# Query projection of the quantised attention layer: whole numbers in one TensorE pass, scales applied afterwards

## The chip, the cores and the metric

The kernel runs on one core of a Trainium2 chip. The metric is the device time of one execution in microseconds (us). Three executions of the kernel before took 3217.35, 3220.0 and 3231.76 us, so the median is 3220.0 us.

## What is computed

The kernel computes a stack of four gated blocks on `x` (2 x 512 tokens, 512 features). Each block adds a cross attention over a context of 2 x 1024 tokens and then a feed-forward layer. The change concerns the third attention layer (L2). There the tokens and the query weights are rounded to 8-bit steps ahead of the product:

```python
def _qdq(x):
    s = jnp.maximum(jnp.max(jnp.abs(x), axis=-1, keepdims=True) / 127.0, 1e-08)
    return jnp.clip(jnp.round(x / s), -127.0, 127.0) * s
q = _qdq(x) @ _qdq(wq).T + bq
kv = cond @ wkv.T + bkv
attn = jax.nn.softmax(jnp.einsum('bnhd,bmhd->bhnm', q, k) * scale, axis=-1)
o = jnp.einsum('bhnm,bmhd->bnhd', attn, v).reshape(B, N, C)
out = _qdq(o) @ _qdq(wp).T + bp
```

Each token has one step `s`, and each output feature of `wq` has one. The rounded values divided by their steps are whole numbers from -127 to 127.

## The kernel before, in words

The layers run one after another. Each is a sequence of blocks, and a block ends when all engines have ended their part of it. For L2 the blocks are the norm (`norm_block`), the attention (`streamed_attention_block`), a turn back to rows (`token_major_block`) and the output (`output_block`).

**The weights' rounding lies far ahead.** In the first layer's attention (`linear_attention_block`) VectorE rounds 128 rows of L2's `wq` and `wp` in each of four rounds with `quantise_rows`. It multiplies the whole numbers by their step again (L1975). TensorE turns them and they go to a scratch in DRAM, `wq_scratch`.

**Norm block of L2.** VectorE takes two tiles of 128 tokens at a time: it normalises them (L178), rounds them with `quantise_rows` (L1970 to L1975) and releases TensorE, which transposes them (L207). ScalarE copies the result into `xT` (L226), which has the features on the partitions. There are 8 tiles, so 4 such pairs.

**Attention block.** It works on 8 sets (4 groups of 4 heads x 2 sequences). In the code `n` is the set. For each set TensorE makes five product items of four chunks each: items 0 and 1 are the keys' halves, 2 is the queries (`QUERIES`), 3 and 4 the values. All go through two banks of `product_ps` in one fixed order. Keys and queries are multiplied as plain float32 (L1391). ScalarE then adds the bias and rounds to the fp32r type (`high`, L1503, into `kh` and `qh`). VectorE takes the remainder (`low`, L1595, into `kl` and `ql`), reading the same bank. SyncE copies the parts into `k_stack` and `q_stack` in SBUF (L1350). Scores are then fp32r products of these stacks.

The instruction streams are written out by hand. A set has 32 units `u`. In each unit TensorE makes one score product (`scores`, L1427), one or two products for the row maxima of the next set (`row`, L1407) and perhaps one chunk for the set two further on (`CHUNK_AT`). After every fourth unit comes the product of probabilities and values (`pv`, L1440). The queries' chunks stand at units 22, 23, 24 and 26 and are the last of a set; ScalarE's `high` of them stands at unit 27 and VectorE's `low` at unit 28. VectorE takes the maximum of each row product (`maximum`, L1601); there are two banks for them, so a row product waits for the maximum two before it. When all 32 are taken, `join` (L1608) reduces them. TensorE turns the result (`turn`, L1414, unit 28), ScalarE and VectorE split it (L1496, L1578), and SyncE copies it into `q_stack` (`fold`, L1357). The next set's first score waits for that copy. ScalarE's other work is one exponential for each score (L1522). GpSimd adds up the probabilities (L1567).

Ahead of the sets the block makes all items of sets 0 and 1 (`FIRST_ITEMS`); the row products of set 0 stand between the chunks of set 1.

## Time and profile before

| | before |
|---|---|
| median of three executions | 3220.0 us |
| the profiled execution | 3227.4 us |
| its span, first to last instruction | 3225.7 us |
| TensorE, VectorE, ScalarE, GpSimd busy | 84%, 54%, 36%, 28% |
| mean granted TensorE clock | 0.921 of 2.4 GHz |
| norm block of L2 | 1532 to 1562.2 us |
| attention block of L2 | 1562.8 to 1994 us |

The profile gives times from the start of the span. PE is TensorE's matmul queue, DVE is VectorE, ACT is ScalarE, POOL is GpSimd, SP is SyncE. A float32 matmul leaves two records, an fp32r one leaves one. Matmuls overlap: the time that one costs in a dense stretch is the distance between the starts of neighbours and not the length of a record. A row ends with the engine's idle time ahead of the work and with what released it, where there was any.

### The profile page before, as it was taken

How to read it: one execution, taken by the hardware profiler on the slowest of the kernel's cores; microseconds unless marked ns; L12 is line 12 of the kernel's file. 1: busy time of each engine (PE TensorE's matmuls, PEld its weight loads, DVE VectorE, ACT ScalarE, POOL GpSimd, SP SyncE). 2: the span in 40 equal slices, each digit the busy share in tenths (PEclk: the TensorE clock that was granted, in tenths of full speed). 3: DMA queues.
4: the chain of work that ended last, by engine and by line, in shares of the span. 5: the costliest groups of instructions: out<-in, count | busy, mean ns of one | idle time of the engine just before them, and what ended most of it. 6: DMA issues, size and time to landing. Idle time of an engine off the chain costs nothing. (4 is left out here: it accounts for less than half of the span.)

```text
span 3225.7 us, 35731 instructions
## 1 busy us (share of the span) xinstructions
PE 2710.5 (84%) x11415; PEld 1641.4 (51%) x11415; DVE 1733.3 (54%) x3048; ACT 1175.1 (36%) x2510; POOL 918.3 (28%) x436
## 2 busy tenths in 40 slices
PE   7998797999764599999699988588589988699895
PEld 3555585644232365565454543266454543477563
DVE  2454675477657899893655653411555653444212
ACT  0111221466625788780144444111134443222110
POOL 0000000488331010100056663112257663221112
PEclk9989898999986799999799998789799997899998
DMA  6220222332200100100332120332532220212623
GB/s 222 80 96 23 72 75 83 92 78 60 53 30 0 53 27 27 52 27 13 103 70 66 34 60 17 139 142 86 148 70 51 49 60 17 79 40 101 207 65 112
DMA packets 101257, 232.26 MB, mean 72 GB/s; under 512 B 22512, under 2 KB 27120, under 8 KB 99696
## 3 DMA queue, kind: packets, MB, share of 16 engines
q1 hardware_dynamic: 88624, 189.46, 19.6%
q0 software_dynamic: 12480, 40.90, 3.8%
q8 instruction: 78, 1.28, 0.2%
q14 instruction: 75, 0.61, 0.1%
HBM read 142.74 MB, written 30.67 MB: 54 GB/s over the span
## 5 line engine op out<-in xcount | busy, mean ns | idle before, releaser
L1567 POOL TENSOR_TENSOR L_attn_total<-L_attn_total,L_attn_probs 128x2048 f32<-128x2048 f32 x120 | 546.3, 4552 | 163.2 <-ACT L_attn_probs L1522 158.9
L1601 DVE TENSOR_REDUCE L_attn_row_max<-L_attn_rows_ps 128x1 f32<-128x512 f32 x512 | 336.9, 684 | 274.6 <-PE L_attn_rows_ps L1407 271.5
L1522 ACT ACTIVATE L_attn_probs<-L_attn_s_ps 128x512 f32<-128x512 f32 x512 | 292.8, 596 | 427.5 <-PE L_attn_s_ps L1427 424.2
L1427 PE MATMUL L_attn_s_ps<-L_attn_q_stack,L_attn_k_stack 98*128 98x512 f32 (+1 forms) x768 | 382.4, 534 | 39.3 <-DMA L_attn_q_stack<-L_attn_ml 33.5
L477 PE MATMUL L_ffn_hidden<-L_ffn_x_high,L_ffn_up_high 128*128 128x512 f32 x688 | 295.2, 429 | 102.6 <-DVE L_ffn_routes L393 54.4
L359 ACT ACTIVATE L_ffn_sums<-sims 128x128 f32<-128x128 f32 x1024 | 315.5, 389 | 47.3 <-DVE L_ffn_routes L379 26.9
L1567 POOL TENSOR_TENSOR L_attn_total<-L_attn_probs 128x2048 f32<-128x2048 f32 x20 | 91.0, 4551 | 796.5 <-ACT L_attn_probs L1522 796.5
L1427 PEld LDWEIGHTS L_attn_s_ps<-L_attn_q_stack,L_attn_k_stack 98*128 98x128 f32 (+1 forms) x768 | 144.1, 197 | 267.7 <-issue 132.4
L477 PE MATMUL L_ffn_hidden<-L_ffn_x_low,L_ffn_up_high 128*128 128x512 f32 x688 | 272.6, 396 | 0.0
L1407 PE MATMUL L_attn_rows_ps<-L_attn_k_stack,L_attn_q_stack 96*128 96x512 f32 x512 | 212.9, 451 | 28.3 <-DVE L_attn_row_max L1601 25.6
L1440 PE MATMUL L_attn_o_ps<-L_attn_probs,L_attn_values 128*32 128x512 f32 x1536 | 212.9, 627 | 27.1 <-ACT L_attn_probs L1522 22.9
L498 PE MATMUL L_ffn_y<-L_ffn_down_in,L_ffn_h 128*128 128x512 f32 x512 | 229.1, 593 | 2.0 <-DVE L_ffn_h L605 2.0
L1522 ACT ACTIVATE L_attn_probs<-L_attn_s_ps,keep_mask 128x512 f32<-128x512 f32 x256 | 186.6, 777 | 93.9 <-DVE L_attn_s_ps L1613 93.4
L1391 PE MATMUL L_attn_product_ps<-L_attn_ctxT,L_attn_wk 128*128 128x512 f32 x384 | 200.4, 616 | 15.7 <-DMA L_attn_ctxT<-in_ctxT 12.1
L1396 PEld LDWEIGHTS L_attn_product_ps<-L_attn_wv,L_attn_ctxT 128*128 128x128 f32 x1536 | 206.7, 200 | 11.1 <-issue 1.7
L477 PEld LDWEIGHTS L_ffn_hidden<-L_ffn_x_high,L_ffn_up_high 128*128 128x128 f32 x688 | 132.2, 192 | 153.3 <-issue 82.0
L1396 PE MATMUL L_attn_product_ps<-L_attn_wv,L_attn_ctxT 128*128 128x128 f32 x1536 | 207.5, 283 | 0.0
L1613 DVE TENSOR_SCALAR L_attn_s_ps<-L_attn_s_ps 128x512 f32<-128x512 f32 x256 | 166.4, 692 | 64.0 <-PE L_attn_s_ps L1427 62.6
L341 POOL TENSOR_TENSOR L_ffn_up_low<-L_ffn_up_in,L_ffn_up_high 128x512 fp32r<-128x512 f32 (+1 forms) x30 | 66.7, 2228 | 457.6 <-ACT L_ffn_up_high L335 457.5
L477 PE MATMUL L_ffn_hidden<-L_ffn_x_high,L_ffn_up_low 128*128 128x512 f32 x432 | 172.1, 398 | 0.0
L1407 PEld LDWEIGHTS L_attn_rows_ps<-L_attn_k_stack,L_attn_q_stack 96*128 96x128 f32 x512 | 101.4, 198 | 116.5 <-DVE L_attn_row_max L1601 83.1
L1036 DVE TENSOR_TENSOR L_ffn_hidden_rows<-L_ffn_silu_out,L_ffn_up_ps 128x256 f32<-128x256 f32 (+1 forms) x46 | 21.7, 471 | 240.7 <-PE L_ffn_up_ps L930 240.7
(276 smaller groups left out, 4321.9 us busy)
## 6 DMA issues: line engine op xcount, KB each, us to landing
L_attn_k_stack<-L_attn_kh SPq DMA_DIRECT2D x192, 128.0 KB, 2.3
L_attn_ctxT<-in_ctxT SPq DMA_DIRECT2D x8, 2048.0 KB, 10.8
L_attn_abs_in<-in_L_ffn_w SPq DMA_DIRECT2D x12, 1024.0 KB, 9.1
L_attn_k_stack<-L_attn_kl SPq DMA_DIRECT2D x96, 128.0 KB, 2.3
L_attn_q_stack<-L_attn_qh SPq DMA_DIRECT2D x192, 64.0 KB, 2.0
L_ffn_xg<-x_slots POOLq DMA_DIRECT2D x46, 256.0 KB, 3.2
y_slots<-L_ffn_y_sb POOLq DMA_DIRECT2D x46, 256.0 KB, 2.3
L_ffn_up_all<-in_L_ffn_w SPq DMA_DIRECT2D x16, 704.0 KB, 12.2
```

The costliest lines, as they stand in the source:

```text
L359: last = nc.scalar.activation(sums[:, h, a * NK:(a + 1) * NK], sims[:, t, h, KEY_ROWS:KEY_ROWS + NK], ACT.Identity, bias=sims[:, t, h, bas ...
L477: last = nc.tensor.matmul(hidden_ps[0:m, b, side, :], w[:, i, e0:e0 + m], x_parts[xp][:, i, h * HALF:(h + 1) * HALF], start=(q == 0), stop ...
L498: last = nc.tensor.matmul(y_ps[:, t % YB, :], h_parts[hp][0:m, s, c, t * P:(t + 1) * P], down_parts[wp][0:m, s, c, :], start=(q == 0), sto ...
L1391: last = nc.tensor.matmul(bank(n, i), w[:, s, c * P:(c + 1) * P], moving, start=(c == 0), stop=(c == DC - 1))
L1396: last = nc.tensor.matmul(bank(n, i)[:, c * P:(c + 1) * P], ctxT[:, d, at:at + P], wv[:, s, d * P:(d + 1) * P], start=(d == 0), stop=(d == ...
L1407: nc.tensor.matmul(rows_ps[:, r % R_SLOTS, :], q_stack[0:FOLD, n % 2, h, q * P:(q + 1) * P], k_stack[0:FOLD, n % 2, h, i * HALF:(i + 1) * ...
L1427: nc.tensor.matmul(s_ps[:, v % S_SLOTS, :], k_stack[0:depth, n % 2, h, kt * P:(kt + 1) * P], q_stack[0:depth, n % 2, h, :], start=True, st ...
L1440: last = nc.tensor.matmul(o_ps[HD * h:HD * (h + 1), :], values[:, n % V_SLOTS, kt, HD * h:HD * (h + 1)], probs[:, g % P_SLOTS, h, :], star ...
L1522: nc.scalar.activation(probs[:, g % P_SLOTS, h, :], s_ps[:, v % S_SLOTS, :], ACT.Exp, **kinds).then_inc(exp_done, 1)
L1567: nc.gpsimd.tensor_tensor(total[:], first, probs[:, g % P_SLOTS], ALU.add).then_inc(added, 1)
L1601: nc.vector.tensor_reduce(row_max[:, r // HALVES_K, r % HALVES_K:r % HALVES_K + 1], rows_ps[:, r % R_SLOTS, :], AX_X, ALU.max, negate=True ...
L1613: nc.vector.tensor_scalar(scores, scores, BOUND / SCALE, -BOUND / SCALE, ALU.min, ALU.max).then_inc(clipped, 1)
```

## The change

- The norm block of L2 leaves `xn` as whole numbers (`whole=(0, 1)`). The tokens' steps are spread over all partitions: VectorE multiplies the identity by each tile's steps (8 small products into `diagonal`), TensorE multiplies a tile of ones by each (8 float32 matmuls of 128x128 into `steps_ps`), and ScalarE copies the two halves into `x_steps`. TensorE's part stands behind all the transposes, ScalarE's behind all copies of `xT`.
- The first layer leaves the rows of `wq` as whole numbers and copies their steps into `q_step`, with one more small VectorE copy in each of four rounds.
- `xT` and the weight tile `wq` have type fp32r in L2, so that the queries' product is an fp32r matmul.
- In L2 a new VectorE instruction, at the place of `low` of the queries, multiplies the product by both steps and writes it to `ql`. ScalarE's `high` waits for it (`q_scaled`) and reads `ql` in place of the bank, as does VectorE's `low`.

The other layers' instructions are as before.

```diff
@@ norm_block, VectorE
-                        quantise_rows(nc, link, xn[:, t % 4:t % 4 + 2, :], xn[:, t % 4:t % 4 + 2, :], top, tmp)
+                        quantise_rows(nc, link, xn[:, t % 4:t % 4 + 2, :], xn[:, t % 4:t % 4 + 2, :], top[:, :, t:t + 2], tmp,
+                                      whole=(0, 1))
                         dve.sem_inc(xn_done, 2)
+                        for u in (t, t + 1):
+                            nc.vector.tensor_scalar(diagonal[:, u, :], env.ident[:], top[:, 0, u:u + 1], None,
+                                                    ALU.mult).then_inc(diagonal_done, 1)
@@ norm_block, TensorE
+                if quantised:
+                    pe.wait_ge(ones_made, 1)
+                    for t in range(TILES):
+                        pe.wait_ge(diagonal_done, t + 1)
+                        last = nc.tensor.matmul(steps_ps[:, t * P:(t + 1) * P], ones[:], diagonal[:, t, :], start=True, stop=True)
+                        if t % 4 == 3:
+                            last.then_inc(spread_done, 1)
@@ norm_block, ScalarE
+                if quantised:
+                    for h in range(HALVES):
+                        act.wait_ge(spread_done, h + 1)
+                        nc.scalar.copy(env.x_steps[:, h * HALF:(h + 1) * HALF], steps_ps[:, h * HALF:(h + 1) * HALF]).then_inc(
+                            steps_copied, 1)
+                    act.wait_ge(steps_copied, HALVES)
@@ streamed_attention_block, ScalarE, high(n, i)
-                    nc.scalar.activation(dst, bank(n, i), ACT.Identity, bias=bias).then_inc(high_done, 1)
+                    product = bank(n, i)
+                    if whole and i == QUERIES:
+                        act.wait_ge(q_scaled, n + 1)
+                        product = ql[:].bitcast(F32)
+                    nc.scalar.activation(dst, product, ACT.Identity, bias=bias).then_inc(high_done, 1)
@@ streamed_attention_block, VectorE, low(n, i)
+                    product = bank(n, i)
+                    if whole and not key:
+                        b, f = n % BATCH, n // BATCH
+                        product = ql[:].bitcast(F32)
+                        dve.wait_ge(product_done, place[n, i] + 1)
+                        if n:
+                            for h in range(HG):
+                                dve.wait_ge(stacked[h], STACKS * n)
+                        nc.vector.scalar_tensor_tensor(product, bank(n, i), env.q_step[:, f:f + 1],
+                                                       env.x_steps[:, b * SEQ:(b + 1) * SEQ], ALU.mult, ALU.mult).then_inc(
+                                                           q_scaled, 1)
+                        dve.wait_ge(q_scaled, n + 1)
                     halves = slice(i * HALF, (i + 1) * HALF) if key else slice(0, SEQ)
                     parts, to = (kh, kl) if key else (qh, ql)
                     dve.wait_ge(high_done, highs[n, i] + 1)
-                    nc.vector.scalar_tensor_tensor(to[:, halves], bank(n, i), (bk if key else bq)[:, n // BATCH % 2, :],
+                    nc.vector.scalar_tensor_tensor(to[:, halves], product, (bk if key else bq)[:, n // BATCH % 2, :],
                                                    parts[:, halves].bitcast(F32), ALU.add, ALU.subtract).then_inc(
                                                        product_free, 1)
@@ linear_attention_block, VectorE
-                    quantise_rows(nc, link, rows_in[:], rows_in[:], rows_top, rows_tmp)
+                    quantise_rows(nc, link, rows_in[:], rows_in[:], rows_top, rows_tmp, whole=(0,))
+                    link(nc.vector.tensor_copy(env.q_step[:, bass.ds(f, 1)], rows_top[:, 0, 0:1]))
@@ build
+                env.xT = sb(f"{name}_xT", [P, DC, TOK], F32R if quantised else F32)
+                env.x_steps = sb(f"{name}_x_steps", [P, TOK]) if quantised else None
```

## Rows read from the trace of the kernel before

**Rows 1.** page, section 1: busy us, share of the span, instructions

```profile
PE 2710.5 (84%) x11415; PEld 1641.4 (51%) x11415; DVE 1733.3 (54%) x3048; ACT 1175.1 (36%) x2510; POOL 918.3 (28%) x436
```

**Rows 2.** stages: from:to, length, busy us (count) by engine, granted clock, DMA share, GB/s

```profile
1530.00:1563.00 33.00, 8.00 (x33) 6.43 (x33) 26.68 (x61) 6.27 (x10) 0.32 (x1) 0.56 0.51 179
...
1563.00:1568.00 5.00, 5.00 (x7) 2.03 (x8) 0.00 (x0) 0.00 (x0) 5.00 (x1) 0.52 0.00 0
...
1606.00:1994.00 388.00, 347.18 (x1658) 180.00 (x1657) 200.78 (x310) 162.18 (x292) 232.98 (x57) 0.94 0.22 51
...
1746.00:1758.00 12.00, 11.59 (x46) 5.20 (x44) 6.78 (x11) 5.12 (x10) 7.71 (x3) 1.00 0.01 1
...
1762.00:1766.00 4.00, 4.00 (x23) 3.47 (x25) 0.00 (x0) 1.23 (x3) 3.86 (x2) 0.57 0.66 152
```

**Rows 3.** waits of TensorE, 1563 to 2000 us: total, times, longest

```profile
PE L_attn_s_ps L1427 <- DMA L_attn_q_stack<-L_attn_ml: 16.8, 8, 3.1
...
PE L_attn_rows_ps L1407 <- DVE L_attn_row_max L1601: 12.9, 35, 1.2
```

**Rows 4.** timeline, TensorE, end of one set: start, length, work [idle before <-releaser]

```profile
1750.30 1.02 PE L1391 MATMUL L_attn_product_ps<-L_attn_xT,L_attn_wq 128*128 128x512 f32 x2
...
1750.75 0.79 PE L1427 MATMUL L_attn_s_ps<-L_attn_q_stack,L_attn_k_stack 98*128 98x512 f32 x1
...
1753.17 0.40 PE L1427 MATMUL L_attn_s_ps<-L_attn_q_stack,L_attn_k_stack 98*128 98x512 f32 x1
...
1753.41 0.40 PE L1407 MATMUL L_attn_rows_ps<-L_attn_k_stack,L_attn_q_stack 96*128 96x512 f32 x1
...
1754.12 0.50 PE L1407 MATMUL L_attn_rows_ps<-L_attn_k_stack,L_attn_q_stack 96*128 96x512 f32 x1 [0.31 <-DVE L_attn_row_max L1601]
...
1754.46 1.02 PE L1391 MATMUL L_attn_product_ps<-L_attn_xT,L_attn_wq 128*128 128x512 f32 x2
...
1756.41 0.49 PE L1427 MATMUL L_attn_s_ps<-L_attn_q_stack,L_attn_k_stack 98*128 98x512 f32 x1
...
1761.56 0.50 PE L1427 MATMUL L_attn_s_ps<-L_attn_q_stack,L_attn_k_stack 98*128 98x512 f32 x1 [2.05 <-DMA L_attn_q_stack<-L_attn_ml]
```

**Rows 5.** timeline, VectorE, the same stretch

```profile
1748.95 0.74 DVE L1595 SCALAR_TENSOR_TENSOR L_attn_kl<-L_attn_product_ps,L_attn_bk,L_attn_kh 128x512 fp32r<-128x512 f32 x1
...
1753.37 1.97 DVE L1601 TENSOR_REDUCE L_attn_row_max<-L_attn_rows_ps 128x1 f32<-128x512 f32 x3 [0.27 <-PE L_attn_rows_ps L1407]
...
1755.38 0.19 DVE L1608 TENSOR_REDUCE L_attn_less_max<-L_attn_row_max 128x16 f32<-128x32 f32 x1
...
1758.14 0.75 DVE L1595 SCALAR_TENSOR_TENSOR L_attn_ql<-L_attn_product_ps,L_attn_bq,L_attn_qh 128x512 fp32r<-128x512 f32 x1 [2.58 <-ACT L_attn_qh L1503]
```

**Rows 6.** timeline, ScalarE, the same stretch

```profile
1756.94 0.60 ACT L1522 ACTIVATE L_attn_probs<-L_attn_s_ps 128x512 f32<-128x512 f32 x1 [2.71 <-PE L_attn_s_ps L1427]
...
1757.43 0.68 ACT L1503 ACTIVATE L_attn_qh<-L_attn_product_ps,L_attn_bq 128x512 fp32r<-128x512 f32 x1
...
1758.48 0.24 ACT L1496 CAST L_attn_mh<-L_attn_product_ps 16x128 fp32r<-16x128 f32 x1
```

**Rows 7.** timeline, end of the quantised layer's norm stage

```profile
1559.65 1.97 PE L207 MATMUL L_attn_turned<-ident,L_attn_xn 128*128 128x128 f32 x8 [3.41 <-DVEq L189]
...
1561.66 0.58 ACT L226 COPY L_attn_xT<-L_attn_turned 128x512 f32<-128x512 f32 x1 [0.27 <-PE L_attn_turned L207]
```

**Rows 8.** instructions by line and shape, VectorE: a small tile

```profile
L1927 DVE TENSOR_TENSOR L_attn_heads<-L_attn_o_ps,L_attn_inv 128x128 f32 x32 | 9.3, 292 | 5.0 <-DVE L_attn_inv L1925 0.3
```

**Rows 9.** timeline, TensorE, first products of the attention stage

```profile
1562.87 9.56 PE L1391 MATMUL L_attn_product_ps<-L_attn_ctxT,L_attn_wk 128*128 128x512 f32 x16 [1.25 <-PEq L142]
...
1572.27 3.60 PE L1391 MATMUL L_attn_product_ps<-L_attn_xT,L_attn_wq 128*128 128x512 f32 x8
...
1575.70 8.20 PE L1396 MATMUL L_attn_product_ps<-L_attn_wv,L_attn_ctxT 128*128 128x128 f32 x72
```

**Rows 10.** timeline, TensorE, first scores of the attention stage

```profile
1614.67 0.80 PE L1427 MATMUL L_attn_s_ps<-L_attn_q_stack,L_attn_k_stack 98*128 98x512 f32 x1 [3.08 <-DMA L_attn_q_stack<-L_attn_ml]
```

More of the change, by code:

```diff
@@ L138, in norm_block @@
         SLOTS = xn.shape[1]
-        top = local.enter_context(nc.sbuf_tensor(f"{name}_norm_top", [P, 2, 2], F32))
+        top = local.enter_context(nc.sbuf_tensor(f"{name}_norm_top", [P, 2, TILES], F32))
+        if quantised:
+            ones = local.enter_context(nc.sbuf_tensor(f"{name}_norm_ones", [P, P], F32))
+            diagonal = local.enter_context(nc.sbuf_tensor(f"{name}_norm_diagonal", [P, TILES, P], F32))
+            steps_ps = local.enter_context(nc.psum_tensor(f"{name}_steps_ps", [P, TOK], F32))
+            diagonal_done, spread_done, steps_copied = (env.sem(n) for n in ("diagonal_done", "spread_done", "steps_copied"))
+            ones_made = env.sem("ones_made")
         tmp = local.enter_context(nc.sbuf_tensor(f"{name}_norm_tmp", [P, 2, D], F32))
@@ L171, in _ @@
                         nc.vector.bn_aggr(meanvar[:, t, :], stats[:, t, :]).then_inc(var_done, 1)
+                if quantised:
+                    nc.vector.memset(ones[:], 1.0).then_inc(ones_made, 1)
                 dve.wait_ge(sd_done, 1)
@@ L208, in _ @@
                     last.then_inc(transposed, 1)
+                if quantised:
+                    pe.wait_ge(ones_made, 1)
[4 more added lines that the diff above has]
+                            last.then_inc(spread_done, 1)
                 if router:
@@ L229, in _ @@
                         nc.scalar.copy(split[0][:, :, cols], env.xT[:, :, cols]).then_inc(high_done, 1)
+                if quantised:
+                    for h in range(HALVES):
[3 more added lines that the diff above has]
+                    act.wait_ge(steps_copied, HALVES)
                 act.wait_ge(copied, TILES)
@@ L1223, with __init__ @@
 class GroupWeights:
-    def __init__(self, env, name, local):
+    def __init__(self, env, name, local, query_dtype):
         def sb(n, shape):
-            return local.enter_context(env.nc.sbuf_tensor(f"{name}_{n}", shape, F32))
+            return local.enter_context(env.nc.sbuf_tensor(f"{name}_{n}", shape, query_dtype if n == "wq" else F32))
         env.prefix = f"{name}_weights"
@@ L1312, in streamed_attention_block @@
     norm_done, added, taken, inverted = env.sem("norm_done"), env.sem("added"), env.sem("taken"), env.sem("inverted")
+    whole, q_scaled = env.x_steps is not None, env.sem("q_scaled")
     with ExitStack() as local:
@@ L1955, in _, with quantise_rows @@
                 dve.wait_ge(step, 3)
-def quantise_rows(nc, link, src, dst, top, tmp):
+def quantise_rows(nc, link, src, dst, top, tmp, whole=()):
     MAGIC = 1.5 * 2 ** 23
@@ L1974, in quantise_rows @@
     link(nc.vector.tensor_scalar(tmp[:], tmp[:], MAGIC + 127.0, MAGIC - 127.0, ALU.min, ALU.max))
-    each(lambda r: nc.vector.tensor_scalar(dst[:, r, :], tmp[:, r, :], -MAGIC, s[:, r:r + 1], ALU.add, ALU.mult))
+    each(lambda r: nc.vector.tensor_scalar(dst[:, r, :], tmp[:, r, :], -MAGIC, *((None, ALU.add) if r in whole else
+                                                                               (s[:, r:r + 1], ALU.add, ALU.mult))))
 def output_block(env, name, heads_out, gate, wo_dram, quantised=False, after_norm=False, feature_major=False, early=None):
@@ L2148, in build @@
         env.iota8 = stack.enter_context(nc.sbuf_tensor("iota8", [P, 8], F32))
-        env.eps_ln = stack.enter_context(nc.sbuf_tensor("eps_ln", [P, 1], F32))
+        columns = stack.enter_context(nc.sbuf_tensor("columns", [P, 1 + D // P], F32))
+        env.eps_ln, env.q_step = columns[:, 0:1], columns[:, 1:]
         abs_sums = stack.enter_context(nc.sbuf_tensor("abs_sums", [P, 3, D // P], F32))
@@ L2172, in attention_layer @@
                 env.io["ctxT"] = io["ctxT"]
-                env.xT, env.ctxT = sb(f"{name}_xT", [P, DC, TOK]), sb(f"{name}_ctxT", [P, DC, BATCH * CTX])
+                quantised = kinds.get("quantised", False)
+                env.xT = sb(f"{name}_xT", [P, DC, TOK], F32R if quantised else F32)
+                env.ctxT = sb(f"{name}_ctxT", [P, DC, BATCH * CTX])
+                env.x_steps = sb(f"{name}_x_steps", [P, TOK]) if quantised else None
                 env.prefix = name
@@ L2179, in attention_layer @@
                 keep_mask = None
-                quantised = kinds.get("quantised", False)
                 if quantised:
@@ L2195, in attention_layer @@
                 else:
-                    weights = GroupWeights(env, name, local)
+                    weights = GroupWeights(env, name, local, F32R if quantised else F32)
                     def first_loads(sp, group):
```

4 lines of the change are left out of this document (2 added, 2 removed).

## The prediction

> **What bounds the kernel now.** I read the page's engine shares first: TensorE is busy 84% of the span, VectorE 54% [rows 1]. That is a mean over eight layers, and the change touches one of them, so the table by stages comes next. In the quantised layer's attention, from 1606 to 1994 us, TensorE is busy 347 of 388 us and no other engine passes 233 [rows 2]. TensorE sets the time there, and the waits say what fills most of its gaps: 16.8 us for the copy of the folded maxima, about 2 us at each set's start, and 12.9 us in 35 short waits for VectorE's row maxima [rows 3]. So a microsecond taken from TensorE inside a set is worth a microsecond, unless VectorE's maxima take over. The norm stage ahead is the opposite: TensorE works 8 of 33 us, at a mean clock of 0.56, and VectorE 26.7 us [rows 2]. Whatever is put behind its last step lengthens it.
>
> **One query chunk.** A float32 chunk is two records. In the first item of queries eight records start from 1572.27 and the next work starts at 1575.70 [rows 9], so a record takes 0.43 us and a chunk 0.86. What an fp32r matmul of the same 512 columns costs, the score and row products show: neighbours start at 1753.17 and 1753.41 [rows 4], 0.24 us. A chunk falls by 0.62 us. Eight sets have 32 chunks, in all 19.8 us of TensorE's time. Not all of it can be kept.
>
> **Six sets in the steady part (2 to 7).** Their queries' chunks stand in units 22 to 26 of the set two before, between 8 row products, each of which needs a maximum. Three maxima take 1.97 us on VectorE [rows 5], 0.66 each. From unit 22 to 26 VectorE has 8 of them and one `low` of the keys of 0.74 [rows 5], 6.0 us. TensorE has 13 score and row products of 0.24 there, four chunks of 0.86 and one `pv`, which with the last chunk takes 1.95 us (1754.46 to 1756.41 [rows 4]), so 1.09 alone; with the 0.31 that row 31 waits that is 8.0 us, and would be 5.5. VectorE is then the longer of the two, but it starts 0.4 us behind the first row and may end 0.9 behind the last chunk, so the two are level. With two banks for the rows I step through the stretch: row 28 waits 0.2 us for maximum 26 (held up by the keys' `low`), rows 30 and 31 wait for the maxima two before, and the last chunk ends 2.35 us earlier instead of 2.5. Row 31 already waits 0.31 us now [rows 4]. I take 2.4 us a set. The lower bound is 1.5 (each row handed over late by a tenth), the upper 2.5. Six sets: 14.4 us, bounds 9 and 15.
>
> **The new step of VectorE, and the wait for it.** It is a scalar_tensor_tensor from PSUM with an SBUF operand, as the remainder is, 0.75 us [rows 5]. Behind the last maximum come `join`, 0.19 [rows 5], and then the scaling. After the change row 31 starts 0.23 us ahead of the last chunk; the last maximum ends about 1.25 us after row 31's start, `join` at 1.45, the scaling at 2.2. Queued behind the wait on ScalarE are exponentials 28 to 31 and the fold's `high`. But ScalarE's exponential 27 stands ahead of it: `pv` (1.09 us) and score 27 follow the last chunk, the exponential starts 0.53 us after score 27 (1756.41, 1756.94) and the queries' `high` 0.49 later [rows 4, 6]. Counted from row 31 that is 0.34 + 0.24 + 1.09 + 0.53 + 0.49 = 2.7 us. The scaling is ready 0.5 us before it is wanted. The cost is nothing; if that cover is gone, up to 0.75 us a set. On VectorE itself the fold's remainder is queued behind the queries' `low`, which starts when `high` has ended (it waits 2.58 us for that now [rows 5]), so it is unchanged. From score 27 on the path to the next set's first score (`high`, `low`, fold, copy, 1756.41 to 1761.56 with 2.05 us of waiting [rows 4]) is what it was. SyncE's copies keep their order.
>
> **Sets 0 and 1.** TensorE is through set 0's queries 2.5 us sooner. The stack's copies follow scaling, `high` and `low` one after the other (0.75 + 0.68 + 0.75), where there were two steps, and the scaling waits for the keys' `low` ahead of it. So the first copy, and with it the first row product, comes about 1.1 us sooner (bounds 0 and 2.5). For set 1 the order turns against the change. Now its `high` is over before VectorE has taken the last maximum; afterwards scaling and `high` both stand behind that maximum, ahead of `low` and `join`. That adds 0.75 + 0.68 us, less 0.4 which the maxima gain, so 1.1 to the wait before the first score, which is 3.08 us now [rows 10] (bounds 0.5 and 1.6). Together 0.
>
> **The norm.** Six of eight diagonals stand ahead of the last transposes. The nearest rows are a 128x128 product, 0.29 us [rows 8], and `join`, 0.19, the smallest here [rows 5]; I take 0.25, so 1.5 us (1.1 to 1.8). The ones' tile fits into the wait for the square root. Behind the last transposes come 8 float32 matmuls of 128 columns, 16 records. At the low clock eight transposes take 1.97 us [rows 7], 0.25 each; dense at full clock 72 records of 128 columns take 8.2 us [rows 9], 0.114 each. So 3.9 or 1.8 us. Then a copy of 0.58 [rows 7] behind some 0.35 us of latency. Now the last copy ends 2.6 us after the transposes begin (1559.65 to 1562.24 [rows 7]); afterwards 1.97 + 3.9 + 0.35 + 0.58 = 6.8, or 4.7. I take 3.5 more (2.1 to 4.2). Something comes back. The first 16 records of the attention block take 1562.87 to 1572.27, 9.4 us [rows 9], at a granted clock of 0.52 in the first 5 us, that is at 1.2 GHz [rows 2]; at full clock they would take 16 x 0.43 = 6.9. TensorE did only short bursts before. After the change it works right through some 5 us and then pauses near 1.5 us, so it may start that block at the upper level: 0 to 2.5 us, I take 1.5. The norm costs 1.5 + 3.5 - 1.5 = 3.5 us, bounds 0.7 and 6.
>
> **At nothing.** The fourfold small copy in the first layer (some 0.2 us each) lies on VectorE where it waits for TensorE; if that cover is gone, 0.8 us. Type changes move no bytes, and the whole numbers' copies and last rounding steps keep their shapes. GpSimd is busy 233 of the 388 us [rows 2] and is not reached.
>
> **Sum.** -14.4 + 0 + 3.5 = -10.9 us. Against the profiled execution (span 3225.7, 3227.4 with what lies around it) that is 3216.5; its time lies 0.2% above the median. Against the median it is 3220.0 - 10.9 = 3209 us.
>
> **Rivals.**
> *All is kept (0.12).* VectorE never holds the rows up, the first copies follow TensorE's full gain, and the clock stays up through the norm: 15 + 1.5 - 0.7 = 16 us, and with the clock falling less often at the sets' starts some 18: 3202. For it: the maxima's waits are short now. Against: row 31 waits already.
> *VectorE takes the stretch over (0.15).* Each row is handed over later than I count and a set keeps 1.5 us: -9 + 4.5 = -4.5, 3215.
> *The scaling comes late: slower (0.06).* If the maxima bound the stretch fully, TensorE's gain becomes wait, and the set's end counts from the last maximum with scaling, `high` and `low` in a row. The decisive point is the 0.5 us of slack above; beyond it each set pays up to 0.75 us, with nothing of the 2.4 us kept: 6 x 0.75 + 1.5 at the start + 6 from the norm = +12, 3232. Against: VectorE waits 2.58 us at this place now [rows 5].
> *The clock gives it back (0.12).* TensorE's clock was full from 1746 to 1758, in the query stretch, and fell to a mean 0.57 from 1762 to 1766, behind the pause of 2.05 us [rows 2, 4]. That is 3.4 us at 1.2 GHz and costs 1.7. If the thinner query stretch brings such a fall to each of six sets, 10 us go: -11 + 10 = -1, 3219. The Trainium skill, "TensorE: Matmul & The Clock Gate", section "A second HAM failure mode: psum-queue depth-cycling", says that brief idling between groups of matmuls makes the clock swing between its levels. By that rule this rival is the likely one; the trace has 0.3 us pauses in the stretch at full clock, so it does not bear it out so far.
> *The product stays at two records (0.02).* Then only costs are left: about 3225.
> The forecast has 0.53.
>
> **How the numbers follow.** 3209 is the likeliest case, and its own range is 3203 to 3214. The range of 3200 to 3220 takes in the first rival, the two that give back and a few microseconds by which the clock's falls elsewhere may shift; late scaling and the two-record case are left out. A measurement can tell about 0.5%, 16 us, from no change, so faster means under 3204 and slower over 3236. Faster: the first rival and the forecast's edge, 0.17. Slower: half of the late scaling and a bad clock, 0.04. Same: 0.79.
>
> **What would show it.** Query records in this layer: 32 in place of 64, neighbours 0.24 us apart. The stretch from unit 22 to score 27 shorter by 2.4 us. The wait for the folded copy still near 2 us a set but above 4 at the first. `high` of the queries still released by score 27's exponential, not by the scaling. The norm's end 5 us later after its last rounding began, the following keys' items 1 to 2.5 us shorter. What would make it wrong: waits for row maxima well above 12.9 us, or a clock under 0.9 in the query stretches.

## The result

The changed kernel takes 3239.05 us (median of five, 3231.08 to 3245.74) against 3220.0 us of the kernel before. The ratio is 1.0059 with a 95% interval of 1.0042 to 1.0076: slower, by 14 to 24 us, where 11 us less were forecast and the range ended at 3220. The profiled execution took 3245.7 us, one of the longer ones of the five.

The page of the changed kernel, its span and engine shares (against [rows 1]):

```profile
span 3243.8 us, 35762 instructions
...
PE 2704.3 (83%) x11399; PEld 1641.7 (51%) x11399; DVE 1762.9 (54%) x3069; ACT 1176.9 (36%) x2512; POOL 919.9 (28%) x436
```

TensorE is busy 6.2 us less, and the span is 18.1 us longer. VectorE is busy 29.6 us more than the 1733.3 of before, and the new instructions do not account for that: 8 scalings of 0.75 and 8 diagonals of 0.25 make 8 us. TensorE's waits from 1568 to 2020 us show where the time stands (against [rows 3]):

```profile
PE L_attn_s_ps L1453 <- DMA L_attn_q_stack<-L_attn_ml: 39.6, 8, 5.9
...
PE L_attn_rows_ps L1433 <- DVE L_attn_row_max L1643: 13.7, 41, 1.2
```

The wait for the folded maxima's copy went from 16.8 to 39.6 us, and its longest from 3.1 to 5.9. The waits for row maxima are 13.7 against 12.9: VectorE did not take the query stretch over. The end of the same set as in [rows 4] to [rows 6], first TensorE:

```profile
1764.97 0.39 PE L1417 MATMUL L_attn_product_ps<-L_attn_xT,L_attn_wq 128*128 128x512 f32 x1
...
1765.21 0.40 PE L1453 MATMUL L_attn_s_ps<-L_attn_q_stack,L_attn_k_stack 98*128 98x512 f32 x1
...
1767.00 0.39 PE L1417 MATMUL L_attn_product_ps<-L_attn_xT,L_attn_wq 128*128 128x512 f32 x1
...
1768.32 0.50 PE L1453 MATMUL L_attn_s_ps<-L_attn_q_stack,L_attn_k_stack 98*128 98x512 f32 x1
...
1777.28 0.79 PE L1453 MATMUL L_attn_s_ps<-L_attn_q_stack,L_attn_k_stack 98*128 98x512 f32 x1 [5.85 <-DMA L_attn_q_stack<-L_attn_ml]
```

A query chunk is one record now and its neighbour starts 0.24 us later (1764.97, 1765.21). Score 27 starts 1.32 us after the last chunk, 1.95 before. From a set's first query chunk to its score 27 TensorE takes 6.47 to 6.53 us in all six sets that have such chunks (0 to 5), and 8.62 to 8.65 before: 2.1 us less a set. Then the next set's first score waits 5.85 us where it waited 2.05. ScalarE and VectorE in that stretch:

```profile
1768.85 0.60 ACT L1552 ACTIVATE L_attn_probs<-L_attn_s_ps 128x512 f32<-128x512 f32 x1 [2.10 <-PE L_attn_s_ps L1453]
...
1769.34 0.71 ACT L1533 ACTIVATE L_attn_qh<-L_attn_ql,L_attn_bq 128x512 fp32r<-128x512 f32 x1
```

```profile
1767.92 0.19 DVE L1650 TENSOR_REDUCE L_attn_less_max<-L_attn_row_max 128x16 f32<-128x32 f32 x1
...
1768.13 0.75 DVE L1630 SCALAR_TENSOR_TENSOR L_attn_ql<-L_attn_product_ps,columns,L_attn_x_steps 128x512 f32<-128x512 f32 x1
...
1770.16 4.43 DVE L1637 SCALAR_TENSOR_TENSOR L_attn_ql<-L_attn_ql,L_attn_bq,L_attn_qh 128x512 fp32r<-128x512 f32 x1 [1.28 <-ACT L_attn_qh L1533]
...
1774.52 0.27 DVE L1608 TENSOR_TENSOR L_attn_ml<-L_attn_product_ps,L_attn_mh 16x128 fp32r<-16x128 f32 x1
```

ScalarE's `high` of the queries (1769.34) follows exponential 27 without a wait, and the scaling (1768.13) is over 0.46 us ahead of it. The row that is new is the third of VectorE's: the remainder of the queries, L1637, is listed for 4.43 us. It took 0.75 [rows 5]. Everything behind it, the fold's remainder at 1774.52 and the two copies of the fold, is late by 3.7 us. GpSimd at that time:

```profile
1769.52 9.43 POOL L1597 TENSOR_TENSOR L_attn_total<-L_attn_total,L_attn_probs 128x2048 f32<-128x2048 f32 x2 [0.61 <-ACT L_attn_probs L1552]
```

It has just begun one of its additions, 0.64 us ahead of the remainder; two of them make 9.43 us, so the first ends near 1774.1 and the remainder half a microsecond later. The queries' remainders of sets 2 to 7, by line (min, median, max in ns):

```profile
L1637 DVE SCALAR_TENSOR_TENSOR L_attn_ql<-L_attn_ql,L_attn_bq,L_attn_qh x6: 4434/4435/4451, 1664.7 to 1927.7; 128x512 fp32r<-128x512 f32 x6
```

There are six of about 4440 ns. The one difference of this instruction from before is its first operand: it reads the scaled product from `ql` in SBUF, not from the PSUM bank. The same instruction for sets 0 and 1 (at 1582.92 and 1617.88), where GpSimd adds nothing yet, takes 0.75 us.

The norm's end and the attention's first products (against [rows 7] and [rows 9]), and three stretches with their granted clock (against [rows 2]):

```profile
1566.09 1.97 PE L219 MATMUL L_attn_turned<-ident,L_attn_xn 128*128 128x128 f32 x8 [3.67 <-DVEq L198]
...
1566.13 0.48 DVE L200 TENSOR_SCALAR L_attn_norm_diagonal<-ident,L_attn_norm_top 128x128 f32<-128x128 f32 x2
...
1567.85 3.62 PE L225 MATMUL L_attn_steps_ps<-L_attn_norm_diagonal,L_attn_norm_ones 128*128 128x128 f32 x16
...
1572.72 7.11 PE L1417 MATMUL L_attn_product_ps<-L_attn_ctxT,L_attn_wk 128*128 128x512 f32 x16 [1.25 <-PEq L148]
```

```profile
1573.00:1578.00 5.00, 5.00 (x13) 2.14 (x12) 0.75 (x1) 0.69 (x1) 5.00 (x1) 1.00 0.00 0
...
1622.00:2013.00 391.00, 331.82 (x1624) 175.98 (x1624) 221.84 (x306) 160.03 (x289) 234.08 (x57) 0.92 0.22 51
...
1777.28:1783.28 6.00, 6.00 (x27) 4.56 (x27) 0.00 (x0) 1.79 (x3) 1.68 (x1) 0.50 0.76 171
```

The norm takes 29.4 us from its square root to the first product, 25.3 before. The first 16 records of the attention take 7.11 us, 9.56 before, since the clock is full there (1.00 against 0.52).

### The profile page after: what moved, and what is told of

The parts are those of the page before. It is cut to its first block and busy times, and to the rows that moved or that the text cites. A ratio compares the mean times of both kernels' runs of the same rounds, so it can differ in the third digit from the quotient of the medians.

```text
span 3243.8 us, 35762 instructions
## 1 busy us (share of the span) xinstructions
PE 2704.3 (83%) x11399; PEld 1641.7 (51%) x11399; DVE 1762.9 (54%) x3069; ACT 1176.9 (36%) x2512; POOL 919.9 (28%) x436
## 5 line engine op out<-in xcount | busy, mean ns | idle before, releaser
L1466 PE MATMUL L_attn_o_ps<-L_attn_probs,L_attn_values 128*32 128x512 f32 x1536 | 215.4, 634 | 26.5 <-ACT L_attn_probs L1552 22.8
```

What stands on the lines that cost most here:

```text
L1466: last = nc.tensor.matmul(o_ps[HD * h:HD * (h + 1), :], values[:, n % V_SLOTS, kt, HD * h:HD * (h + 1)], probs[:, g % P_SLOTS, h, :], star ...
```

## The experiments

**Theory A:** the remainder waits for GpSimd's addition under way, because two SBUF inputs take VectorE through a read path that GpSimd uses as well. **Theory B:** the wait is longer because scaling, `high` and `low` stand in a row. The clock was looked at as well, since it decides what is left of the gain.

Two notions are used below. "The layer" is L2's attention from its norm's square root to that of the next norm, on ScalarE's timeline. "The sets" run from the first score to the turn back to rows. Sets 0 to 5 hold the queries' chunks of sets 2 to 7; sets 6 and 7 hold none, so the two groups are listed apart. All figures are us.

| kernel | layer | norm | first product to first score | sets | of these sets 0 to 5 | sets 6 and 7 | wait for the fold's copy | time |
|---|---|---|---|---|---|---|---|---|
| before | 514.8 | 25.3 | 51.8 | 379.6 | 296.1 | 83.5 | 16.8 | 3220.0 |
| before, second trace | 516.4 | 25.2 | 52.5 | 381.1 | 298.6 | 82.4 | - | - |
| before, third trace | 509.3 | 25.2 | 51.5 | 374.1 | 295.2 | 78.8 | - | - |
| changed | 527.2 | 29.4 | 49.5 | 390.7 | 312.6 | 78.2 | 39.6 | 3239.1 |
| changed, second trace | 526.6 | 29.3 | 49.1 | 390.5 | 312.4 | 78.1 | 39.7 | - |
| e1_bank | 503.5 | 29.4 | 49.1 | 366.9 | 288.8 | 78.1 | 17.6 | 3218.5 |
| e1_bank, second trace | 503.2 | 29.4 | 49.1 | 366.8 | 288.6 | 78.2 | - | - |
| e2_write_only | 510.4 | 29.3 | 49.7 | 373.8 | 286.2 | 87.6 | 17.4 | 3222.4 |
| e3_halves | 517.6 | 29.3 | 49.4 | 381.4 | 301.5 | 79.9 | 26.7 | 3228.7 |
| e4_bank_spread | 503.3 | 26.8 | 52.1 | 366.5 | 288.3 | 78.1 | 17.6 | 3217.8 |
| f4_bank_f32 | 520.1 | 29.4 | 51.3 | 380.4 | 297.6 | 82.8 | 19.4 | 3230.0 |
| g1_warm | 502.9 | 25.6 | 49.1 | 369.3 | 288.6 | 80.7 | 18.8 | 3215.4 |
| g2_double | 506.2 | 29.3 | 50.6 | 368.0 | 289.2 | 78.8 | 18.9 | - |

### e1_bank: the scaled queries stay in their PSUM bank

```diff
@@ ScalarE, high(n, i)
                     if whole and i == QUERIES:
                         act.wait_ge(q_scaled, n + 1)
-                        product = ql[:].bitcast(F32)
@@ VectorE, low(n, i)
-                        product = ql[:].bitcast(F32)
                         dve.wait_ge(product_done, place[n, i] + 1)
-                        if n:
-                            for h in range(HG):
-                                dve.wait_ge(stacked[h], STACKS * n)
```

> The changed kernel, but the scaled queries go back into their PSUM bank, and ScalarE's high and VectorE's low read the bank. Theory A (operands): low waits for GpSimd's addition because both its inputs lie in SBUF. Then low falls from 4.43 to 0.75 us, the wait for the folded copy at a set's start from 5.85 to near 2.0, in all 39.6 to 17 us, and the time to 3239 - 23 less 2 to 6 for a clock that stays up: 3208 to 3216. Theory B (the added step): the path is longer because scaling, high and low stand in a row. Then wait and time stay, 3235 to 3243, with low long or not.

Measured: 3218.5 us, ratio to before 0.9993 (0.9978 to 1.0007). The remainder by line, and the wait:

```profile
L1632 DVE SCALAR_TENSOR_TENSOR L_attn_ql<-L_attn_product_ps,L_attn_bq,L_attn_qh x7: 749/752/752, 1616.6 to 1906.4; 128x512 fp32r<-128x512 f32 x7
```

```profile
PE L_attn_s_ps L1453 <- DMA L_attn_q_stack<-L_attn_ml: 17.6, 8, 3.1
```

The three steps still stand in a row, and the whole of the new wait is gone: Theory B falls. The layer is 23.7 us shorter than the changed kernel's. The time is 20.5 us lower, but it ends 2.5 us above the range that was expected. That range counted 2 to 6 us for a clock that stays up, and in the sets it does not (see below).

### e2_write_only: GpSimd works as before, but reads nothing

The additions of the probabilities in this layer are replaced by three fills of the same tile each (the softmax sums of sets 0 to 6 are left out; GpSimd has 147 fills in place of 49 additions).

```diff
-                            nc.gpsimd.tensor_tensor(total[:], first, probs[:, g % P_SLOTS], ALU.add).then_inc(added, 1)
+                            if whole:
+                                for part in range(2):
+                                    nc.gpsimd.memset(total[:], 1.0).then_inc(filled, 1)
+                                    fills[0] += 1
+                                    pool.wait_ge(filled, fills[0])
+                                nc.gpsimd.memset(total[:], 1.0).then_inc(added, 1)
+                            else:
+                                nc.gpsimd.tensor_tensor(total[:], first, probs[:, g % P_SLOTS], ALU.add).then_inc(added, 1)
```

> The changed kernel with low reading SBUF twice, but in this layer GpSimd's additions of the probabilities are replaced by three fills of the same tile, which only write (the softmax sums of six sets are then not computed, so that GpSimd's reads are the part left out). Theory A, a read path that the two engines share: low 0.75 us, the wait near 2.0, time 3208 to 3217. Variant A2, any work of GpSimd blocks VectorE: low between 0.75 and 2.5 us according to where a fill stands, the wait 2 to 4. Theory B: no change in the wait, 5.85.

Measured: 3222.4 us, 1.0011 (0.9995 to 1.0026). By line and by wait:

```profile
L1645 DVE SCALAR_TENSOR_TENSOR L_attn_ql<-L_attn_ql,L_attn_bq,L_attn_qh x7: 751/752/754, 1615.1 to 1902.3; 128x512 fp32r<-128x512 f32 x7
```

```profile
PE L_attn_s_ps L1454 <- DMA L_attn_q_stack<-L_attn_ml: 17.4, 8, 3.1
```

The remainder still reads SBUF twice and takes 0.75 us. One pair of rows, GpSimd's and VectorE's, shows that both work at once:

```profile
1756.23 3.67 POOL L1600 MEMSET L_attn_total<- 128x2048 f32 x2
```

```profile
1756.40 0.75 DVE L1645 SCALAR_TENSOR_TENSOR L_attn_ql<-L_attn_ql,L_attn_bq,L_attn_qh 128x512 fp32r<-128x512 f32 x1 [1.29 <-ACT L_attn_qh L1534]
```

A pair of fills is under way at each of the six. So it is not GpSimd's being at work, nor its writing, that holds VectorE up (variant A2 falls). What is left is what the additions do beyond that, and their reading is the plain candidate. The time missed the expected 3208 to 3217. Sets 0 to 5 are the shortest of all (286.2 us), but sets 6 and 7 take 87.6 us where the changed kernel has 78.2, at a granted clock of 0.74 in set 6 against 0.85. There TensorE also waits 4.0 us for fills, three of which take 5.4 us where one addition takes 4.6.

### e3_halves: each addition as two instructions

```diff
-                            nc.gpsimd.tensor_tensor(total[:], first, probs[:, g % P_SLOTS], ALU.add).then_inc(added, 1)
+                            if whole:
+                                two = HG // 2
+                                nc.gpsimd.tensor_tensor(total[:, :two], first[:, :two], probs[:, g % P_SLOTS, :two], ALU.add)
+                                nc.gpsimd.tensor_tensor(total[:, two:], first[:, two:], probs[:, g % P_SLOTS, two:],
+                                                        ALU.add).then_inc(added, 1)
+                            else:
+                                nc.gpsimd.tensor_tensor(total[:], first, probs[:, g % P_SLOTS], ALU.add).then_inc(added, 1)
```

> The changed kernel, but each of GpSimd's additions in this layer is split into two instructions of half the size. Theory A: low waits for the instruction under way only. One starts 0.6 us ahead of low and takes about 2.3, so low is 2.4 to 2.6 us in place of 4.43, the wait for the copy near 3.9 in place of 5.85, and the time 3239 - 12 = 3222 to 3229. If VectorE has to wait for GpSimd's whole run of work, low stays at 4.4 or more. Theory B: no change.

Measured: 3228.7 us, 1.0028 (1.0016 to 1.004). By line, by wait, and one pair of rows:

```profile
L1643 DVE SCALAR_TENSOR_TENSOR L_attn_ql<-L_attn_ql,L_attn_bq,L_attn_qh x7: 752/2290/2303, 1611.0 to 1911.9; 128x512 fp32r<-128x512 f32 x7
```

```profile
PE L_attn_s_ps L1453 <- DMA L_attn_q_stack<-L_attn_ml: 26.7, 8, 3.7
```

```profile
1758.17 2.39 POOL L1599 TENSOR_TENSOR L_attn_total<-L_attn_total,L_attn_probs 128x1024 f32<-128x1024 f32 x1 [0.45 <-ACT L_attn_probs L1552]
...
1760.50 2.80 POOL L1600 TENSOR_TENSOR L_attn_total<-L_attn_total,L_attn_probs 128x1024 f32<-128x1024 f32 x1
```

```profile
1758.80 2.30 DVE L1643 SCALAR_TENSOR_TENSOR L_attn_ql<-L_attn_ql,L_attn_bq,L_attn_qh 128x512 fp32r<-128x512 f32 x1 [1.29 <-ACT L_attn_qh L1533]
```

The remainder is 2.30 us and ends 0.54 us after the half that was under way (1758.17 + 2.39). VectorE waits for one GpSimd instruction and then goes ahead; the second half is listed with 2.80 us, where a half without a remainder beside it takes 2.37. The longest wait of TensorE is 3.7 us, as expected (3.9).

With these three, the runs show Theory A's rule: a remainder with two SBUF inputs waits until the GpSimd addition under way is over, and does not wait beside fills. That the cause is a shared read path is what a page states; no run here looks inside. The Trainium skill, page "SBUF — State Buffer", section "Who interferes with whom", says that a VectorE instruction with two SBUF inputs contends with a GpSimd instruction that reads SBUF, since its second input comes through the shared read interface, and not with one that only writes it. Its section "SBUF: two separate sides" adds that who starts first has the shared ports for its whole instruction and that the other is fully blocked. The runs here agree: 0.75 us beside fills, 4.43 beside a whole addition, 2.30 beside a half.

### f4_bank_f32: e1_bank without the single pass

```diff
-                env.xT = sb(f"{name}_xT", [P, DC, TOK], F32R if quantised else F32)
+                env.xT = sb(f"{name}_xT", [P, DC, TOK], F32)
-                    weights = GroupWeights(env, name, local, F32R if quantised else F32)
+                    weights = GroupWeights(env, name, local, F32)
```

> As e1_bank, but xT and wq stay plain float32, so that the queries' chunks go back to two records. It measures the gain from one pass alone. By the prediction's steps six sets keep 2.4 us each and the start about 1: the sets take 366.9 + 14.4 = 381 us and the whole 3218.5 + 15 = 3234 us. Rival: if VectorE's maxima bound the stretch, a set keeps 1.5 us or less, and the time is 3218.5 + 9 = 3227 or less.

Measured: 3230.0 us, 1.0037 (1.0022 to 1.0051), so the one pass is worth 11.5 us in time (14 by the ratios to before, which were taken on two occasions). The sets take 380.4 us against 366.9, which is 13.5 us less for e1_bank. But only 8.8 of these lie in sets 0 to 5 (297.6 against 288.8), which hold the chunks. The other 4.7 lie in sets 6 and 7, whose instructions are the same in both kernels: 1.8 are the wait at the last set's start (3.2 against 1.4), the rest goes with the granted clock in set 7 (0.84 against 0.99). So it is chance that 13.5 comes near the expected 14.4. The expected time, 3234, is not met, nor is the rival's 3227. The 8.8 us are 1.5 a set, which is the rival's number, but not by its cause: from first query chunk to score 27 a set takes 8.63 us here and 6.50 in e1_bank, so the pass gives 2.1 us a set, and TensorE's waits for row maxima are 13.8 us here and 13.4 there. What takes the rest back is the clock at the sets' starts, next.

### The clock: two more traces of before, and f3_bank

The kernel before and e1_bank were traced again, without an edit.

> The kernel before again, for a second trace: how long is its quantised attention layer, and the layers around it, from one execution to the next? If its first trace is typical, that layer again takes 514.8 us (from its norm's square root to the next layer's) and e1_bank's 503.5 us is a gain of 11.3, as the prediction's sum has it. If it was one of the slow ones, the layer takes 505 to 510 us and most of e1_bank's gain in that comparison is the clock's chance.

> A third trace of the kernel before, with the same two expectations as f1_before: 514.8 us for the quantised attention layer, or 505 to 510.

> A second trace of e1_bank. If the layer's length is a matter of instructions and not of the clock, it is 503.5 us again, within 1.5.

Measured: the layer of before takes 516.4 and 509.3 us beside the first trace's 514.8, that of e1_bank 503.2 beside 503.5. So e1_bank gains 10 us in the layer on the mean of three, 6 on the best of them. Both expected cases for before occur, near 514.8 twice and in 505 to 510 once; e1_bank's length holds within the 1.5 us expected.

The first six microseconds of sets 1 to 6, behind TensorE's pause for the folded maxima, show where the clock falls (the last three columns are granted clock, DMA share and GB/s). Kernel before, first trace:

```profile
1662.63:1668.63 6.00, 6.00 (x32) 4.59 (x33) 0.00 (x0) 1.97 (x4) 5.13 (x2) 0.72 0.72 161
...
1712.89:1718.89 6.00, 6.00 (x46) 4.75 (x46) 0.00 (x0) 3.46 (x6) 5.16 (x2) 1.00 0.76 171
...
1761.56:1767.56 6.00, 6.00 (x32) 4.54 (x33) 0.00 (x0) 1.96 (x4) 5.14 (x2) 0.72 0.77 173
...
1811.86:1817.86 6.00, 6.00 (x46) 4.75 (x46) 0.00 (x0) 3.46 (x6) 5.15 (x2) 1.00 0.77 172
...
1860.52:1866.52 6.00, 6.00 (x32) 4.54 (x33) 0.00 (x0) 1.99 (x4) 5.13 (x2) 0.72 0.61 137
...
1910.77:1916.77 6.00, 4.85 (x25) 1.99 (x29) 1.29 (x2) 4.24 (x8) 5.17 (x2) 0.93 0.77 172
```

And e1_bank, first trace:

```profile
1667.03:1673.03 6.00, 6.00 (x27) 4.57 (x27) 0.00 (x0) 1.79 (x3) 5.04 (x2) 0.50 0.64 142
...
1716.59:1722.59 6.00, 6.00 (x32) 4.25 (x33) 0.00 (x0) 2.01 (x4) 5.08 (x2) 0.72 0.76 171
...
1764.78:1770.78 6.00, 6.00 (x32) 4.54 (x33) 0.00 (x0) 1.97 (x4) 5.04 (x2) 0.72 0.76 171
...
1813.02:1819.02 6.00, 6.00 (x32) 4.74 (x33) 0.00 (x0) 1.96 (x4) 5.06 (x2) 0.72 0.77 172
...
1861.28:1867.28 6.00, 6.00 (x32) 4.69 (x33) 0.00 (x0) 2.03 (x4) 5.06 (x2) 0.72 0.63 141
...
1909.77:1915.77 6.00, 6.00 (x17) 2.84 (x17) 0.44 (x1) 3.30 (x7) 4.70 (x2) 0.50 0.76 171
```

In this trace of before the clock falls at every other set, to a mean of 0.72 (in the second at four of the six, in the third at every other again); in e1_bank it falls at every set, to 0.72 or 0.50, and in its second trace in the same way, within 0.01. Time at 1.2 GHz costs half of itself where TensorE sets the pace: a set of before that starts with 0.72 takes 50.3 us and one that starts with 1.00 takes 48.7. 6 x (1 - clock), summed over the six, is 5.5 us for the first trace of before (8.0 and 5.0 in the others) and 12.7 for e1_bank. f4_bank_f32, whose six pauses are e1_bank's (2.12 to 2.13 us, and one of 2.49), has 7.2. So it is not the length of the pause that brings the additional falls. What differs between these two is the one pass and the 2.1 us by which a set's query stretch is shorter; why that brings a fall at each start is not shown. For the starts of sets 0 to 5 alone the sum is 12.1 us in e1_bank and 7.9 in f4_bank_f32. These 4.2 us are, within the rounding, what lies between the 12.8 us that six shorter query stretches give and the 8.8 us that sets 0 to 5 keep. Like with like, sets that start with 0.72, it is 50.4 us in f4_bank_f32 and 48.2 in e1_bank. In the changed kernel, with pauses of 5.85 us, the sum over the six is 14.6.

The difference between before's traces is another one. Sets 0 to 5 take 296.1, 298.6 and 295.2 us. Sets 6 and 7 take 83.5, 82.4 and 78.8 us. The whole of set 6, first and third trace of before and then e1_bank:

```profile
1910.77:1957.98 47.21, 41.44 (x137) 16.18 (x137) 25.02 (x38) 18.95 (x34) 32.46 (x9) 0.71 0.22 51
```

```profile
1908.18:1948.66 40.48, 34.91 (x137) 13.40 (x138) 24.41 (x38) 18.57 (x34) 31.82 (x9) 0.87 0.26 59
```

```profile
1909.77:1951.08 41.31, 36.19 (x138) 14.38 (x138) 24.46 (x38) 18.58 (x34) 31.56 (x9) 0.84 0.26 58
```

In the first two traces of before TensorE runs at 1.2 GHz for some 24 us of set 6 (47.2 and 46.3 us), in the third it does not (40.5). Set 6 holds no query chunk, and in both traces of e1_bank and of the changed kernel it takes 41.3 to 41.5 us. So of the 10 us that e1_bank gains on the mean, some 3.5 lie in sets 6 and 7, and no run shows that they belong to the change: the third trace of before is within 0.7 us of e1_bank there.

### e4_bank_spread and g1_warm: the norm, and what the clock takes for it

e4_bank_spread is e1_bank with the spreading matmuls of a pair of tiles behind the pair's transposes; g1_warm adds empty matmuls in the gaps. ScalarE's two copies of the spread steps move with them, and the loop behind all transposes goes; neither is shown.

```diff
@@ TensorE, norm_block, in the loop over the tiles
+                    if quantised and t % 2:
+                        if t == 1:
+                            pe.wait_ge(ones_made, 1)
+                        for u in (t - 1, t):
+                            pe.wait_ge(diagonal_done, u + 1)
+                            last = nc.tensor.matmul(steps_ps[:, u * P:(u + 1) * P], ones[:], diagonal[:, u, :], start=True,
+                                                    stop=True)
+                        if t % 4 == 3:
+                            last.then_inc(spread_done, 1)
@@ g1_warm only, behind these
+                        for _ in range(4 if t < TILES - 1 else 1):
+                            nc.tensor.matmul(warm_ps[:, 0:P], ones[:], env.ident[:], start=True, stop=True)
```

> As e1_bank, and in the norm stage the matmuls that spread the tokens' steps stand behind each pair's transposes, where TensorE waits 3.7 us for VectorE, instead of behind them all. 12 of 16 records of 0.226 us leave the end of the stage: 2.7 us less than e1_bank. If the clock then no longer starts the attention's first products at full speed, up to 2.4 us of it is given back. Time 0 to 3 us under e1_bank's under either theory of the sets.

> As e4_bank_spread, with some empty work for TensorE in the norm stage: four float32 matmuls of 128 columns (8 records, 2 us at the low clock) in each gap between pairs and one behind the last, into a PSUM bank that nobody reads. In e4_bank_spread the norm was 2.6 us shorter than in e1_bank (26.8 against 29.4), but the first 16 records of the attention took 9.6 us in place of 7.1, and the two kernels were equal. If it is the clock that takes that back, the first records take 7.1 us here with a norm of at most 26.8, and the layer 2.5 us less than e4_bank_spread's 503.3. If the empty matmuls only get in the way, the norm is longer than 26.8 and nothing is gained.

Measured: e4_bank_spread 3217.8 us, 0.999 (0.9976 to 1.0004), g1_warm 3215.4 us, 0.9979 (0.9966 to 0.9993). g1_warm is the one kernel here whose interval lies under before's time; it is not shown to be faster than e1_bank, since the intervals of the two overlap. TensorE at the end of the norm and behind it, e4_bank_spread and then g1_warm:

```profile
1560.58 1.06 PE L226 MATMUL L_attn_steps_ps<-L_attn_norm_diagonal,L_attn_norm_ones 128*128 128x128 f32 x4
...
1562.89 9.58 PE L1419 MATMUL L_attn_product_ps<-L_attn_ctxT,L_attn_wk 128*128 128x512 f32 x16 [1.25 <-PEq L148]
```

```profile
1561.44 0.61 PE L227 MATMUL L_attn_steps_ps<-L_attn_norm_diagonal,L_attn_norm_ones 128*128 128x128 f32 x4
...
1561.89 0.39 PE L232 MATMUL L_attn_warm_ps<-ident,L_attn_norm_ones 128*128 128x128 f32 x2
...
1563.42 7.11 PE L1422 MATMUL L_attn_product_ps<-L_attn_ctxT,L_attn_wk 128*128 128x512 f32 x16 [1.15 <-PEq L149]
```

e4_bank_spread's norm is 2.6 us shorter and its first 16 records take 9.58 us at the low clock in place of 7.11: all given back. With the empty work the clock is up when the attention begins, the last transposes and spreads run at it too, and norm and start together (25.6 + 49.1 us) are 3.8 us shorter than e1_bank's. The layer, however, is only 0.4 us shorter than e4_bank_spread's, where 2.5 were expected (502.9 against 503.3): the sets took 2.8 us more in that one trace, nearly all of it in sets 6 and 7 (80.7 against 78.1), with 1.2 more waiting for the fold.

### g2_double: how much slack the scaling has

```diff
-                                                           q_scaled, 1)
+                                                           q_once, 1)
+                        dve.wait_ge(q_once, n + 1)
+                        nc.vector.tensor_scalar(bank(n, i), bank(n, i), 1.0, None, ALU.mult).then_inc(q_scaled, 1)
```

> As e1_bank, with a second, empty scaling behind the first (a multiplication by one in the same bank, about 0.7 us). The prediction has the scaling ready 0.5 us before ScalarE wants it; in e1_bank's trace it ends at 1760.0 and high starts at 1760.57. Then high comes 0.1 to 0.3 us later and the wait for the folded copy grows by as much, in all from 17.6 to 18 to 20 us. If the scaling were on the path already, it grows by 0.7 us a set, to 22.

Measured, in one execution: the wait is 18.9 us, 1.3 more than e1_bank's, 0.2 a set. VectorE's two scalings and ScalarE's `high`:

```profile
1752.13 0.75 DVE L1625 SCALAR_TENSOR_TENSOR L_attn_product_ps<-L_attn_product_ps,columns,L_attn_x_steps 128x512 f32<-128x512 f32 x1
...
1752.92 0.70 DVE L1629 TENSOR_SCALAR L_attn_product_ps<-L_attn_product_ps 128x512 f32<-128x512 f32 x1
```

```profile
1753.73 0.69 ACT L1532 ACTIVATE L_attn_qh<-L_attn_product_ps,L_attn_bq 128x512 fp32r<-128x512 f32 x1 [0.18 <-DVE L_attn_product_ps L1629]
```

0.70 us more work on VectorE make `high` wait 0.18 us: the slack was 0.5 us, as the prediction had it. The wait of 18.9 lies in the expected 18 to 20 and under the 22 of a scaling on the path.

### g3_after: the changed kernel again

> The changed kernel again, for a second trace: the remainder of the queries at 4.43 us in six sets and a wait of 39.6 us in all, whatever the clock. The layer took 527.2 us in the first trace, where the clock was among the lowest; here 520 to 527.

Measured: 526.6 us for the layer and a wait of 39.7 us, with six remainders near 4.44 us again. What the first trace shows is the kernel's and not that execution's.

## Why the prediction was wrong

**The step that failed** is the one sentence on VectorE: "the fold's remainder is queued behind the queries' `low`, which starts when `high` has ended (...), so it is unchanged". What lies ahead of it is unchanged, `low`'s own length is not. The text priced `low` by its row of before, 0.75 us, whose first operand came from PSUM, while the diff gives it one from SBUF. The same error stands under "At nothing", where GpSimd is "not reached": it was only asked for its busy share (233 of 388 us [rows 2]) and not for what it does at that moment. The runs show 4.43 us in place of 0.75. Six sets times 3.7 us are 22 us, and the measured wait grew by 22.8. With the operand back in PSUM (e1_bank) the wait is 17.6 us, and all but 0.8 of the growth is gone.

**The chunk** was right: one record, 0.24 us behind its neighbour, 32 records fewer in the layer. **The six sets** were right in mechanism and a little high in size. The stretch from first query chunk to score 27 is 2.1 us shorter a set, 12.8 us in all, where 2.4 and 14.4 were forecast with bounds of 9 and 15. VectorE's maxima do not bound it (13.4 us of such waits in e1_bank's trace, 12.9 before). What sets 0 to 5 keep of it is 8.8 us by f4_bank_f32, and that step is the clock's. **The scaling's cost of nothing**, with 0.5 us of slack, was right by g2_double. The slower rival, "the scaling comes late", named the right place, the fold's path, but the wrong mechanism; its 3232 is near 3239 by chance.

**Sets 0 and 1** were put at 0. From first product to first score the changed kernel takes 49.5 and 49.1 us against 51.5 to 52.5, and the clock's gain at the first products alone is 1.5 to 2.7, so they are 0 within 1 us. The two opposite terms of 1.1 us that made up this 0 are not what was measured: the first wait is 3.08 again and not above 4, and with plain float32 chunks (f4_bank_f32, first products at full clock too) the stretch takes 51.3 us, so one pass saves about 2.2 us there and the scaling costs nearly as much. The sum was right, its parts were not. **The norm** was forecast at 3.5 us net. Its stage grew by 4.1 where 5.0 were reckoned: 0.7 ahead of the last transposes in place of 1.5, since each rounding's last step became cheaper (0.76 for two tiles in place of 0.88) while the diagonals cost 0.24 each, and 3.4 behind them in place of 3.5. The clock gave back 2.4 where 1.5 were reckoned. Net 1.7, within the bounds.

**The clock rival** named the right place, the sets' starts. In e1_bank a fall does come at each of the six, while the query stretch stays at full clock (1.00 from 1752 to 1762 us). Its price of 10 us counted six new falls of 1.7, though before has three or four of them already; measured are 4 us over sets 0 to 5. With this, e1_bank, which is the kernel that the sum described, gains 10 us in the layer on the mean of before's three traces, near the forecast 10.9, but partly by luck: 3.5 of them lie in sets 6 and 7, where before's first two traces lose time to the clock and its third does not. Against the third trace the gain is 6. In time it is 2 us, with an interval from 7 less to 2 more, which does not reach the forecast 11 less. How the 2 us come out of the layer's 6 to 10 is within what the layers around vary by, and not shown.

**Not settled.** The layers around this one differ by up to 12 us between traces of kernels whose code there is the same (2703.3 to 2715.5 us over e1_bank and its variants, 2705.2 to 2710.9 for before). In the two traces of the changed kernel they take 2716.6 and 2714.3, some 8 us more than before's mean of 2707.4. It is not the change's code there: e2_write_only and e3_halves have the same code in those layers and take 2709.9 and 2705.1. The first layer, with its small copies, is 0.7 us longer on the mean of ten traces (319.0 us, 318.3 before). No run tells the rest apart. Nor does a run show what brings the clock down at a set's start or in set 6.

## What to carry to other kernels

When an edit moves an operand from PSUM to SBUF, count the SBUF inputs of each VectorE instruction that reads it, and look at what GpSimd does at that moment: with two of them it stood still here until GpSimd's addition was over, and the profile lists that as a long instruction and not as a wait. A value that VectorE makes and reads again can often stay in its PSUM bank. And where TensorE pauses in each round, compare the granted clock behind the pauses before a gain is counted in full. Compare rounds with the same instructions first, and look at rounds that the change does not touch: what differs there is not the change's.

## What the runs showed of the hardware that was not expected

- Two SBUF inputs on VectorE, a 128x512 scalar_tensor_tensor, beside GpSimd: 0.75 us beside fills or with GpSimd idle, 2.30 beside an addition of 2.39, 4.43 beside one of 4.52. It ends about 0.5 us after the addition each time.
- A scaling in place within a PSUM bank takes 0.75 us, as from PSUM to SBUF.
- Behind the same pause of 2.12 us the clock falls at six of six set starts in e1_bank (both traces) and at four of six in f4_bank_f32, which differs by the float32 chunks alone; behind 2.05 us before, at three or four of six.
- The same instructions can take 40.5 or 47.2 us from one execution to the next by the granted clock alone (set 6 of before, 0.87 and 0.71).
- Empty matmuls in the gaps of a stage whose bound is VectorE bring the clock up for the next one: 7.11 us in place of 9.58 for 16 records, with a stage that is no longer for them (25.6 us against 26.8).
